# A sparse expert stage on one core: two of twelve row-tile loads split into halves over both queues

## The reference

```python
score = softmax(xf @ Wg + bg);  gate = max(score);  idx = argmax(score)
pos = running count of the tokens that chose the same expert
keep = pos < cap                      # cap = 1216 / 16 = 76
buf[idx, pos] += xf where keep        # 16 experts x 76 rows
h = relu(buf @ W1[e] + b1[e])         # 256 -> 1024
y = h @ W2[e] + b2[e]                 # 1024 -> 256
out = y[idx, pos] * gate where keep   # added to the residual h
```

## Time and profile before

| what | value |
|---|---|
| median of 3 runs | 342.17 us (341.46 to 342.28) |
| profiled execution, its own time | 340.43 us |
| its span, first to last instruction | 338.5 us |
| mean granted TensorE clock in the span | 0.982 of full speed |
| TensorE busy | 321.4 us, 95% of the span |
| ScalarE busy | 172.0 us, 51% |
| VectorE busy | 193.6 us, 57% |
| DMA | 61.05 MB, mean 180 GB/s |

### The profile page before, as it was taken

How to read it: one execution, slowest core, us unless ns; L and a number is a source line. 1 busy time by engine, 2 the same in 40 slices (tenths; PEclk the granted TensorE clock), 3 DMA queues, 4 the chain that set the end, 5 groups by cost and what they waited for, 6 DMA issues and landing times.

```text
span 338.5 us, 8877 instructions
## 1 busy us (share of the span) xinstructions
PE 321.4 (95%) x3254; PEld 235.2 (69%) x3254; DVE 193.6 (57%) x525; ACT 172.0 (51%) x485; POOL 132.2 (39%) x245
## 2 busy tenths in 40 slices
PE   4988999999999999999999999889999999999993
PEld 3877768888888788887888888785464464464461
DVE  4467999546558957676675998821261351351350
ACT  0869925565457765566766574601450450450440
POOL 1166887624428643654834626530002012012012
PEclk9999999999999999999999999859999999999998
DMA  7999900000000071317001118939999998974300
GB/s 228 411 396 410 424 37 24 25 14 24 25 17 19 18 252 26 137 26 251 23 20 54 50 44 264 386 109 383 380 393 367 351 395 307 353 288 146 113 10 13
DMA packets 38234, 61.05 MB, mean 180 GB/s; under 512 B 10591, under 2 KB 29000, under 8 KB 37840
## 3 DMA queue, kind: packets, MB, share of 16 engines
q1 hardware_dynamic: 33912, 51.14, 42.9%
q10 hardware_dynamic: 2632, 7.10, 5.5%
q0 software_dynamic: 1648, 2.24, 1.9%
HBM read 54.21 MB, written 8.48 MB: 185 GB/s over the span
## 4 chain that ended last, share of the span: by engine, by line
PE 83%; DVE 5%; ACT 4%; POOL 3%; issue 2%; DMA 1%; DVEq 0%; POOLq 0%
PE bank L1106 13%; PE bank L1073 13%; PE bank L959 9%; PE bank L1012 6%; PE bank L1028 5%; PE bank L999 5%; PE bank L989 5%; PE bank L970 5%; PE bank L1084 4%; PE bank L1035 3%; PE bank L1112 3%; PE bank L944 3%; PE bank L1018 2%; PE bank L893 1%; POOL rs L826 1%
## 5 line engine op out<-in xcount | busy, mean ns | idle before, releaser
L860 POOL DMA_INDIRECT out<-mid,idx x12 | 11.7, 978 | 98.5 <-DVE mid L1488 98.5
L841 POOL TENSOR_TENSOR mid<-mid,tab 128x608 f32<-128x608 f32 x32 | 38.5, 1209 | 25.7 <-PE bank L989 14.1
L1106 PE MATMUL bank<-early,mid 128*64 128x256 f32 (+1 forms) x448 | 43.7, 381 | 0.0
L1392 DVE TENSOR_REDUCE mx<-bank 102x16 f32<-102x608 f32 x32 | 25.1, 784 | 30.0 <-PE bank L989 29.8
L1269 ACT ACTIVATE mid<-bank,cols 128x64 f32<-128x64 f32 (+1 forms) x128 | 25.9, 333 | 25.1 <-PE bank L1084 25.1
L1073 PE MATMUL bank<-early,mid 128*64 128x512 f32 (+1 forms) x192 | 36.2, 596 | 0.7 <-ACT mid L1252 0.7
L1106 PEld LDWEIGHTS bank<-early,mid 128*64 128x64 f32 (+1 forms) x448 | 25.3, 123 | 15.8 <-issue 2.9
L959 PE MATMUL bank<-xnT,attn 128*128 128x256 f32 (+1 forms) x160 | 34.9, 371 | 0.7 <-DVE attn L1347 0.7
L959 PEld LDWEIGHTS bank<-xnT,attn 128*128 128x128 f32 x160 | 29.0, 190 | 4.4 <-issue 1.3
L826 POOL TENSOR_TENSOR rs<-rs,mhalf 128x1 f32<-128x1 f32 (+2 forms) x50 | 29.8, 596 | 4.2
L825 POOL TENSOR_SCALAR rs<-mv 128x1 f32<-128x1 f32 (+2 forms) x50 | 12.2, 243 | 40.3 <-DVE mv L1307 38.6
(11 more groups left out here) (154 smaller groups left out, 631.6 us busy)
## 6 DMA issues: line engine op xcount, KB each, us to landing
early<-in_w SPq DMA_DIRECT2D x52, 512.0 KB, 7.8
expert_in<-k_empty SPq DMA_DIRECT2D x6, 514.0 KB, 26.5
early<-in_xf SPq DMA_DIRECT2D x4, 768.0 KB, 16.2
early<-in_xt ACTq DMA_DIRECT2D x4, 768.0 KB, 23.0
xnT<-in_w SPq DMA_DIRECT2D x4, 512.0 KB, 7.9
tokens<-in_w SPq DMA_DIRECT2D x4, 512.0 KB, 8.9
attn<-in_w SPq DMA_DIRECT2D x4, 512.0 KB, 8.8
mid<-expert_in SPq DMA_DIRECT2D x6, 257.0 KB, 6.5
```

What stands on the lines that cost most here:

```text
L841: eng.tensor_tensor(km[:, n % 2], bc(kT[:, :, n * PCOLS:(n + 1) * PCOLS], 2, 4), bc(bc(quarterm[:, :], 2, PCOLS), 1, KC), ALU.mult).then_i ...
L1106: ins = mm(Yp[m % 2][a * width:(a + 1) * width, 0:DIM], hT[:, m % 2, c, a * width:(a + 1) * width], w2s[e % W2_SLOTS][:, c, :], start=c == ...
L1392: link(eng.tensor_reduce(mxv, sv, AX.X, ALU.max))
```

## The change

A new helper `half_rows` loads 64 of a tile's 128 rows. SP issues the first halves of tiles 0 and 2, ACT the second halves of both, ahead of everything else that they load. Then SP loads tiles 4, 6, 8, 10 and ACT tiles 1, 3, 5, 7, 9, 11. A semaphore counts 16 for each DMA, so that who reads tile 0 or 2 now waits for 32.

```diff
@@ -669,6 +669,11 @@
+        def half_rows(queue, t, half):
+
+            at = 128 * xrow[t] + 64 * half
+            queue.dma_start(xe[64 * half:64 * half + 64, t, :], xbuf[at:at + 64, :]).then_inc(xe_loaded[t], 16)
+
@@ -762,7 +767,9 @@
             sp.wait_ge(scattered, 16 * TILES)
 
-            for t in range(0, XTILES, 2):
+            half_rows(sp, 0, 0)
+            half_rows(sp, 2, 0)
+            for t in range(4, XTILES, 2):
                 sp.dma_start(xe[:, t, :], xbuf[128 * xrow[t]:128 * xrow[t] + 128, :]).then_inc(xe_loaded[t], 16)
@@ -1051,7 +1058,7 @@
             def turn(ps, t):
-                pe.wait_ge(xe_loaded[t], 16)
+                pe.wait_ge(xe_loaded[t], 32 if t in (0, 2) else 16)
@@ -1244,6 +1251,8 @@
             act.wait_ge(scattered, 16 * TILES)
+            half_rows(act, 0, 1)
+            half_rows(act, 2, 1)
             for t in range(1, XTILES, 2):
                 act.dma_start(xe[:, t, :], xbuf[128 * xrow[t]:128 * xrow[t] + 128, :]).then_inc(xe_loaded[t], 16)
@@ -1477,7 +1486,7 @@
-                dve.wait_ge(xe_loaded[t], 16)
+                dve.wait_ge(xe_loaded[t], 32 if t in (0, 2) else 16)
```

## The result

Over 22 runs each the median went from 341.65 to 342.94 us. The changed kernel takes 1.0041 of the time of before, with a 95% interval of 1.0021 to 1.0061 (the quotient of the two medians is 1.0038). That is 1.4 us (0.7 to 2.1) slower, where no change was forecast. The profiled execution took 341.14 us, of which 339.2 are its span.

A forecast was written before the change was run, and what follows sets the result against it. TensorE was taken as the bound, with L1112 covering the loads. 340.43 us profiled plus 0 for halves, ACT's issues and queue places gave 340.43; with the timed runs' 1.74 us above it, median 342.17 (rounded 342.2), range 341.3 to 343.0.

The forecast's parts named there:

- The bound: At the first turn: TensorE busy for 95% of the span, and tile 0 landed 1.3 us before L1112 ends at 231.12.
- The halves: Loads of tiles 0 and 2: tile 0 lands at 228.8 to 229.1 instead of 229.8; worth nothing on the path.
- 0 for ACT's issues: Ahead of ACT's copy at 231.38: eight issues end at 230.7, so the two added ones cost 0 us.
- The upper bound: ACT's eight issues at 0.70 us each take 5.6 us, ending at 232.1; 0.7 us on the path.
- the whole rival of a late ACT: ACT's eight issues end after its copy is due: slower, 342.9 to 345.9 us; chance 0.09.
- my own signs for this rival: ACTq or an "issue" piece between L1056 and ACT's copy, and eight issues over more than 4.8 us.
- my limit of 0.3 us: Prediction wrong if end of L1112 to the second group at 258.04, 26.92 us, changes by more than 0.3 us.
- My second rival: L1112 ends earlier in timed runs (227.3), exposing the loads; copy 0.6 us later, 342.8 us; chance 0.06.
- Later places in the queue: Tiles 1, 3, 5 to 11 later in ACT's queue: tile 1 lands about 232, margin 1.7 to 3.5 us; cost nothing.
- SP's weights: Behind SP's six loads: expert 4's first weights land at 241.0, used at 258.04, 17 us to spare.
- the waits for 32: Waiting for 32 instead of 16 costs nothing; TensorE's wait is met over a microsecond before it is reached.

The follow-up runs named there:

- the profile of the second series: Changed kernel run again unaltered as an anchor: 1.0022 of before; its profiled execution took 345.80 us, with ACT's last issue ending at 5.76 us.
- profile 2: Further profile of the unaltered changed kernel: copy starts 5.35 us after the first load's issue, rest of the span 112.5 us.
- profile 3: Another profile of the unaltered changed kernel, low clock for 6.8 us: copy starts at 5.71 us, rest of the span 112.9 us.
- profile 3 of before: Further profile of the unaltered kernel before, low clock for 6.8 us: copy starts at 4.35 us, rest of the span 111.5 us.
- changed with 22: Changed kernel with 22 instead of 29 constant multiplications ahead of the first turn: 1.0068 of before (1.0032 to 1.0103).
- ten issues: Changed kernel with tiles 9 and 11 also loaded in halves by ACT: 1.0132 of before (1.0094 to 1.0170).
- five issues and 22: Changed kernel with tiles 7, 9 and 11 behind ACT's first staging copy and 22 constant multiplications: 0.9995 of before (0.9969 to 1.0020).
- the pair with VectorE copying: Changed kernel with 22 constant multiplications, tile 0's turn copied by VectorE instead of ScalarE: 1.0002 of before, against 1.0068 with ScalarE.
- the old order: Kernel before, tiles 0 and 2 whole on SP, but ACT's tiles 9 and 11 in halves, eight ACT issues: 0.9994 of before (0.9967 to 1.0022).
- all halves on SP: Changed kernel with all four halves of tiles 0 and 2 issued by SP, ACT back to six issues: 1.0061 of before (1.0029 to 1.0093).
- Before with 22: Kernel before with 22 instead of 29 constant multiplications ahead of the first turn: 0.9997 of before (0.9976 to 1.0018).
- VectorE copying with 22: Changed kernel with VectorE copying tile 0's turn and 22 constant multiplications: 1.0002 of before (0.9976 to 1.0027).

## Why the prediction was wrong

**The bound was read rightly.** Tile 0 is not waited for in before, in any of three profiles, and bringing it sooner was worth nothing.

**The number.** The median of 342.94 us lies inside the forecast's range of 341.3 to 343.0. That is luck: the range was laid around 342.17 us, the median of three runs, and over 22 runs before has 341.65. For the 1.74 us between the profiled execution and those three, which the forecast left unexplained, the profiles show a place ahead of the change: before's first load is issued at 226.54 and 226.62 us in the profiles of 340.43 and 340.54 us, and at 229.40 us in the one of 342.81 us.

**The halves: over-sized, without effect.** I had tile 0 at 228.8 to 229.1, 0.7 to 1.0 us sooner. It was 0.1 us sooner: 3.2 us after the issue against 3.3. Tile 2, which I had about 2 us sooner, was complete 5.1 us after the first issue instead of 5.4. The 0.7 to 1.0 us were read off the spacing of later landings (2.1 and 1.5 us for each 514 KB), and the first landing did not become shorter by it. The fit from the Trainium skill, DMA: Bandwidth & Descriptors, section "Anatomy of one DMA — SWDGE (gpsimd) path", gave 2.6 us as an estimate for one tile's bytes; one half did land at 2.7, the other, which completes the tile, at 3.2.

**The step that failed** is "With two of the eight at 0.59 and six at 0.49 ACT ends at 226.54 + 4.13 = 230.7, which I take". This is the term "0 for ACT's issues" of the sum. The eight take 5.0, 5.3 and 5.7 us in the first three profiles and 5.8 us in the profile of the second series, not 4.1. The two halves take 0.52 and 0.86 us, 1.4 for both against my 1.2; of the six whole tiles behind them one takes 0.8 to 1.3 us instead of 0.49, and the others up to 0.73. The upper bound that I wrote down, 5.6 us from the slowest issues at the start, was nearly right, and two of the four profiles pass it; I had called it the end of the range, and the whole rival of a late ACT had 0.09. The six of before end after 2.95 to 2.97 us in all three profiles. Of my own signs for this rival, the eight issues over more than 4.8 us are there, and ACTq stands right ahead of the copy in the chain. The stretch from the end of L1112 to the second group, 26.92 us in before, is 27.06 us in the first profile of the changed kernel, 27.33 in profile 2 and 28.25 in profile 3: in the first profile alone the change stays within my limit of 0.3 us.

**The cover was read off a favourable execution.** What hides ACT's issues is the time until L1112 and the turn are over. I weighed them against a copy at 231.38, 4.8 us after the first issue. In profile 3 of before the copy starts at 4.35, as L1112 takes 8.86 us there and not 9.37. My second rival pointed this way, L1112 ending earlier and ACT's added issues taking back more than the halves give, with a copy 0.6 us later. But it had the clock high throughout, L1112 at 5.5 us and tile 0 waited for, none of which any profile shows. I gave it 0.06, and argued that the low clock is part of every execution. It is, but its length is not. A late ACT and an earlier turn come together here, and the copy is 1.4 us late in profile 3.

**The sum.** The first three profiles of the changed kernel have their copy at 5.37 us on average, those of before at 4.69: 0.7 us, at the low end of the measured 0.7 to 2.1. A second drop of the clock behind the gap, 1.6 to 1.7 us each time, was seen with gaps of 2.5 and 2.7 us (changed with 22, ten issues), and in one profiled execution of the changed kernel itself, at 345.8 us, with a gap of 2.0 us. It wasn't seen in the first three profiles, with gaps up to 1.8 us. With that fourth execution the rest of the span averages 113.05 us against 111.8 in before, 1.2 us more, near the 1.4 us of the timed runs. This is an estimate from four profiles and three. How often the drop happens in the timed runs, and so how the loss divides between it and the wait alone, stays open.

**Later places in the queue, SP's weights, the waits for 32** cost nothing, as forecast. Tile 1 landed 7.0 us after the first issue, where I took 5.5 and had 7.3 as the worst, and was there 2.0 us before the turns of tiles 2 and 1 began. From the first product on, the chain of the changed kernel has the same pieces in the same lengths as before, to the second group at 258.74, 26.2 us after 232.50, as 258.04 is 26.2 us after 231.81. The late bias lands later (DVE waits 3.1 us for it instead of 2.1) and that too stays beside the path; it comes onto it only with five issues and 22.

**What is shown and what is argued.** That the copy waits for ACT's issues, and that this costs the time, is shown by the chain and by the pair with VectorE copying. Why ACT's sixth or seventh issue takes 0.7 to 1.4 us with the halves in front is not. SP's issues of the weights begin at about that time in the changed kernel, but two runs speak against them as the sole cause: with the old order ACT's last two of eight issues overlap them at 0.62 us each, and with all halves on SP ACT's sixth takes 0.85 us and is over 1.6 us before they begin. That a queue was full, as I supposed of SP's issue of 4.39 us, is shown by no row.

**A better version?** None beats the kernel before by more than its interval. Before with 22 (0.9997), five issues with 22 (0.9995) and VectorE copying with 22 (1.0002) start the first product 0.4 to 1.1 us earlier by their profiles, which a total of 341 us with this spread doesn't resolve. Two of the reasons are above: 0.3 us more outside the span in the first and the last, and with five issues the wait for the late bias.

## What to carry to other kernels

An engine that issues DMAs and computes pays for each issue in its own order: ask what is queued behind the issues, by when it is due, and put there only those loads that are due first; the others can go behind the first compute step or to an engine with nothing due. Splitting a transfer over two queues halves its bytes on each but adds an issue, and here, at 257 KB with more loads behind, the issue (0.5 us and more) costs more than the landing gains (0.1 us). A margin read from one profile (here 231.38 less 230.7, 0.7 us) is worth a second profile where TensorE's clock changes inside it.

## What the runs showed of the hardware

- A load of 64 rows x 514 floats took 0.52 to 0.86 us to issue, one of 128 rows 0.35 to 0.58 us in the three profiles of before: half the bytes, no cheaper issue.
- Both halves on one queue completed a 257 KB tile 5.2 us after the first issue (all halves on SP), one half on each queue 3.2 us (changed), the tile whole on one queue 3.3 us (before).
- Eight issues in a row on ACT took 4.4 us in one order (whole tiles first, halves last; one profile) and 5.0 to 5.8 us in the other (eight profiles).
- SP's fifth issue of weights behind the row tiles took 3.1 to 5.6 us in each of the 17 profiles of the table. What sets it is not known.
- The Trainium skill, DMA: Bandwidth & Descriptors, section "Issuing engines are not separate DMA queues", calls the time to initiate usually small against the DMA. For one load the trace agrees, 0.52 us against 3.2 us; eight issues in a row (5.0 to 5.8 us) outlast the landing that is waited for.
- In three profiles TensorE stood still for 2.0, 2.5 and 2.7 us ahead of the first product, and its granted clock was at the lower level (1.2 GHz) for about 3.4 us of what followed. In the other profiles of the table it stood still there for 0.5 to 1.8 us, and the clock stayed at 2.4 GHz.
